# Windowed attention moved from stretches of its own into the slots of the expert stream, in a one-core hybrid block

## What is computed

```python
def attn_b(x, w_qkv, w_out, b_out):                    # H = 16 heads of 8, WINDOW = 64
    q, k, v = heads(split(x @ w_qkv.T))
    scores = q @ k.T / sqrt(8)
    allowed = (j <= i) & (i - j < WINDOW)
    attn = softmax(where(allowed, scores, -inf))
    return (attn @ v) @ w_out.T + b_out

def ffn(x):                                            # 32 experts, 8 of them weighted above zero per token
    w = normalised_top8(softmax(x @ gate_w.T))
    gate, up = split(x @ gate_up_w[e].T)               # 64 hidden features of each expert e
    return sum_e w[:, e] * ((silu(gate) * up) @ down_w[e].T)
```

## Time and profile before

| what | value |
|---|---|
| time, median of 3 runs (lowest, highest) | 999.18 us (999.04, 1001.05) |
| span of the profiled execution | 997.6 us |
| PE busy, share of the span | 911.7 us, 91% |
| DVE, ACT, POOL busy | 65%, 61%, 66% |
| the chain that ended last: PE, ACT, POOL, issue, DVE | 61%, 11%, 7%, 5%, 4% |

### The profile page before, as it was taken

How to read it: one execution, slowest core, us unless ns; L and a number is a source line. 1 busy time by engine, 2 the same in 40 slices (tenths; PEclk the granted TensorE clock), 3 DMA queues, 4 the chain that set the end, 5 groups by cost and what they waited for, 6 DMA issues and landing times.

```text
span 997.6 us, 16805 instructions
## 1 busy us (share of the span) xinstructions
PE 911.7 (91%) x5472; PEld 627.0 (63%) x5472; DVE 647.7 (65%) x1447; ACT 611.6 (61%) x1875; POOL 661.2 (66%) x610
## 2 busy tenths in 40 slices
PE   3267899899999999999999999999999998999998
PEld 1144566686666666586666666677666666657665
DVE  5886867688658638697739737787735347437432
ACT  4345566984664575895674575797455377386432
POOL 7676878657688649666759857756765545646554
PEclk8567999989999999999999999999999999999999
DMA  5005252014353524610433534520333560350452
GB/s 185 0 3 135 46 129 72 16 45 108 88 127 87 121 79 96 155 44 12 96 87 88 127 98 85 146 65 18 84 99 81 139 156 12 84 132 12 85 129 63
DMA packets 64762, 85.68 MB, mean 86 GB/s; under 512 B 5218, under 2 KB 30627, under 8 KB 64419
## 3 DMA queue, kind: packets, MB, share of 16 engines
q1 hardware_dynamic: 64674, 84.62, 35.2%
HBM read 79.32 MB, written 5.28 MB: 85 GB/s over the span
## 4 chain that ended last, share of the span: by engine, by line
PE 61%; ACT 11%; POOL 7%; issue 5%; DVE 4%; DVEq 0%; ACTq 0%; POOLq 0%
PE bank L1545 16%; PE bank L1522 8%; PE bank L1524 8%; PE bank L1523 8%; ACT probs L1089 5%; PE bank L1581 4%; PE bank L1566 4%; POOL work L881 3%; PE bank L1595 2%; PE bank L1559 1%; PE bank L1405 1%; POOL kv_terms L846 1%; DVE probsT L1345 1%; PE bank L1399 1%; POOL rstd L833 1%
## 5 line engine op out<-in xcount | busy, mean ns | idle before, releaser
L881 POOL TENSOR_TENSOR work<-work,spread_w 128x512 f32<-128x512 f32 x256 | 336.3, 1325 | 165.4 <-DVE work L1303 162.3
L1303 DVE TENSOR_TENSOR work<-work,bank 128x512 f32<-128x512 f32 x256 | 173.6, 681 | 214.0 <-ACT work L1064 128.1
L1545 PE MATMUL bank<-work,down_w 128*128 128x512 f32 x512 | 263.9, 599 | 9.3 <-POOL work L881 7.4
L1064 ACT ACTIVATE work<-bank 128x512 f32<-128x512 f32 x256 | 151.2, 596 | 182.1 <-PE bank L1524 178.6
L1089 ACT ACTIVATE probs<-bank,neg_max 128x96 f32<-128x96 f32 x512 | 166.0, 382 | 8.2 <-DVE neg_max L1331 5.7
L1522 PE MATMUL bank<-z_hi,gate_hi 128*128 128x512 f32 x256 | 167.0, 652 | 3.6 <-ACT elu L974 2.0
L889 POOL TENSOR_TENSOR probs<-probs,prob_inv 128x768 f32<-128x768 f32 x64 | 94.1, 1470 | 74.0 <-DVE prob_inv L1339 74.0
L1089 ACT ACTIVATION_READ_ACCUMULATOR probs<-bank,neg_max 128x1 f32 x512 | 125.6, 248 | 0.0
L1545 PEld LDWEIGHTS bank<-work,down_w 128*128 128x128 f32 x512 | 94.6, 189 | 40.5 <-POOL work L881 15.0
L1524 PE MATMUL bank<-z_hi,gate_lo 128*128 128x512 f32 x256 | 102.4, 400 | 0.0
L1522 PE MATMUL bank<-z_hi,up_hi 128*128 128x512 f32 x256 | 102.0, 398 | 0.0
(11 more groups left out here) (154 smaller groups left out, 1466.2 us busy)
## 6 DMA issues: line engine op xcount, KB each, us to landing
spread_w<-comb_dram SPq DMA_DIRECT2D x96, 512.0 KB, 6.7
spread_w<-comb_dram SPq DMA_DIRECT2D x128, 128.0 KB, 3.0
vals<-v_dram SPq DMA_DIRECT2D x16, 384.0 KB, 4.1
x_buf<-x SPq DMA_DIRECT2D x8, 256.0 KB, 3.4
v_dram<-v_tok SPq DMA_DIRECT2D x8, 256.0 KB, 4.5
out<-xs SPq DMA_DIRECT2D x8, 256.0 KB, 3.8
spread_w<-wg SPq DMA_DIRECT2D x1, 1024.0 KB, 6.5
spread_w<-wu SPq DMA_DIRECT2D x1, 1024.0 KB, 8.5
```

What stands on the lines that cost most here:

```text
L881: pool.tensor_tensor(work[:, n % WORK], work[:, n % WORK], spread_w[:, n // EACH % 2, s % EACH], ALU.mult).then_inc(hid_gated, 1)
L1064: act.activation(work[:, n % WORK], bank[GATE_BANKS[ring_of(row, f, s)]], ACT.Silu).then_inc(silu_ready, 1)
L1303: dve.tensor_tensor(work[:, n % WORK], work[:, n % WORK], bank[UP_BANKS[ring_of(row, f, s)]], ALU.mult).then_inc(gated_ready, 1)
L1545: pe.matmul(bank[Y_BANK], down_w[:, c], work[:, n % WORK], start=(c == 0), stop=(c == CH - 1)).then_inc(down_done, 1)
```

## The change

The attention stretches are gone. Each tile of attention B is cut into six parts, and a tile takes six consecutive slots of the stream, a new tile beginning every second slot: scores of head groups 0 and 1 with their maxima and the first group's exponentials; scores of groups 2 and 3, exponentials of groups 1 and 2, the first half's transpose; exponentials of group 3, the second half's transpose, the inverse sums; the first mixing phase; the second; the addition on POOL. Only row 0's tiles stand in eight slots without a chunk (`alone`), which take over that stretch's steps; rows 1 and 2 begin in slot 6 of `fourth`, row 3 in slot 4 of `third` and slot 9 of `fourth`. `PLAN` is re-timed around that.

Slots that hold attention (`HELD`, 71 of those with a chunk) use gate bank 4 and up bank 5 alone; the others keep the ring of three. In the 61 slots in which exponentials run, Silu becomes Tanh, which is in one table set with Exp: x·sigmoid(x) = 0.5·x·(1 + tanh(x/2)). In the 32 even ones (`SOFT`) DVE makes two instructions of it; in the 29 odd ones (`COPIED`) DVE makes one, ACT copies half the up bank out, and POOL multiplies by that copy before it multiplies by the weights.

Inside a tile, PE works with 32 x 32 tiles of its array (`tile_position` with four rows and four columns of tiles): scores take keys that are masked per head (`head_keys`) against 32 queries, so that a pair of groups is 8 masks and 8 products of 384 columns; and the mixing takes 24 products of 32 x 32 weights and 128 columns in each of two phases. DVE turns the probabilities itself in blocks of 32 x 32 (`dve.transpose`, 128 x 768, twice), so that PE's transposes and DVE's copies go. The probabilities stay unnormalised: DVE inverts the sums spread over features (128 x 128), PE transposes that, DVE copies it (`inv_turned`), and POOL multiplies the mixed values with it. The values come in 48 loads of 128 KB instead of 16 of 384 KB. Over the whole program PE loses 512 transposes and gains 32; table loads on ACT go from 65 to 56.

The diff, cut:

```diff
+RUNS = [((0, "alone", 0), 0, 0, TILES), ((1, "fourth", 6), 1, 0, TILES), ((2, "fourth", 6), 2, 0, TILES),
+        ((3, "third", 4), 3, 0, T), ((3, "fourth", 9), 3, T, TILES)]
...
+BESIDE = [{} for _ in TIMELINE]
+HELD, SOFT, COPIED = set(), [], []
+for run_start, run_row, run_first, run_end in RUNS:
+    for run_tile in range(run_first, run_end):
+        for stage_of_tile in range(6):
+            BESIDE[SLOT_AT[run_start] + 2 * (run_tile - run_first) + stage_of_tile][stage_of_tile] = run_row, run_tile
+for slot_at, (_, slot_place, slot_row, slot_f, slot_s) in enumerate(TIMELINE):
+    if any(k in BESIDE[slot_at] for k in range(5)):
+        HELD.add(slot_at)
+    if slot_place != "alone" and any(k in BESIDE[slot_at] for k in range(3)):
+        (COPIED if slot_s % 2 else SOFT).append(STAGE_AT[slot_row, slot_f] * CH + slot_s)
...
+        RING[slot_chunk] = 2
+        if slot_at not in HELD:
+            plain.append(slot_chunk)
+    if slot_at in HELD or slot_at == len(TIMELINE) - 1:
+        for back_to_end, plain_chunk in enumerate(reversed(plain)):
+            RING[plain_chunk] = (1, 0, 2)[back_to_end % 3]
...
+                if place == "alone":
+                    send_values(0, 1)
+                    load_windows(0, 2)
+                    next_weights(STAGE_AT[1, 0])
...
                 pool.wait_ge(gated_ready, n + 1)
-            def normalise(row, i, half):
-                pool.tensor_tensor(pr, pr, prob_inv[:, i % 2, part].unsqueeze(2).broadcast_to([P, HALF_BLOCKS, KW]),
-                                   ALU.mult).then_inc(probs_normed, 1)
+                if n in COPIED:
+                    pool.wait_ge(up_copied, COPIED.index(n) + 1)
+                    pool.tensor_tensor(inner, inner, up_copy[:], ALU.mult).then_inc(up_gated, 1)
+                    pool.wait_ge(up_gated, COPIED.index(n) + 1)
+                pool.tensor_tensor(inner, inner, weights, ALU.mult).then_inc(hid_gated, 1)
...
+                pool.wait_ge(mix_taken, 2 * tile(row, i) + 2)
...
+                pool.tensor_tensor(mixT[:, i], mixT[:, i], inv_turned[:], ALU.mult).then_inc(mix_picked, 1)
...
+                inner, gate = work[:, n % WORK], bank[GATE_BANKS[RING[n]]]
+                if n in SOFT or n in COPIED:
+                    act.activation(inner, gate, ACT.Tanh, scale=0.5).then_inc(silu_ready, 1)
+                else:
+                    act.activation(inner, gate, ACT.Silu).then_inc(silu_ready, 1)
+                if n in COPIED:
+                    act.wait_ge(up_ready, n + 1)
+                    wait(act, up_gated, COPIED.index(n))
+                    act.activation(up_copy[:], bank[UP_BANKS[RING[n]]], ACT.Copy, scale=0.5).then_inc(up_copied, 1)
...
+                    silu(row, f, s)
+                if 2 in BESIDE[at]:
+                    exponentials(*BESIDE[at][2], 3)
+                if 0 in BESIDE[at]:
+                    exponentials(*BESIDE[at][0], 0)
+                if 1 in BESIDE[at]:
+                    exponentials(*BESIDE[at][1], 1)
+                    exponentials(*BESIDE[at][1], 2)
...
+                if n in COPIED:
+                    dve.scalar_tensor_tensor(out=inner, in0=inner, scalar=1.0, in1=gate, op0=ALU.add,
+                                             op1=ALU.mult).then_inc(gated_ready, 1)
+                elif n in SOFT:
+                    dve.scalar_tensor_tensor(out=inner, in0=inner, scalar=1.0, in1=gate, op0=ALU.add,
+                                             op1=ALU.mult).then_inc(tanh_gated, 1)
+                    dve.wait_ge(tanh_gated, SOFT.index(n) + 1)
+                    dve.wait_ge(up_ready, n + 1)
+                    dve.scalar_tensor_tensor(out=inner, in0=inner, scalar=0.5, in1=up, op0=ALU.mult,
+                                             op1=ALU.mult).then_inc(gated_ready, 1)
+                else:
+                    dve.wait_ge(up_ready, n + 1)
+                    dve.tensor_tensor(inner, inner, up, ALU.mult).then_inc(gated_ready, 1)
...
-            def turned(row, i, blocks):
-                wait(dve, mix_ready, tile(row, i))
-                for b in blocks:
-                    dve.wait_ge(probsT_ready, tile(row, i) * NB + b + 1)
-                    dve.tensor_copy(probsT[:, b], bank[4 + b % 2][0:KW, :]).then_inc(probsT_copied, 1)
...
+                part = slice(half * HALF_HEADS, (half + 1) * HALF_HEADS)
+                dve.transpose(probsT[:, i % 2, part].rearrange("p h k -> p (h k)"),
+                              probs[:, part].rearrange("p h k -> p (h k)")).then_inc(probs_turned, 1)
...
+                dve.reciprocal(prob_inv[:].rearrange("p (h d) -> p h d", d=HD),
+                               prob_sum[:, i % 2].unsqueeze(2).broadcast_to([P, H, HD])).then_inc(inv_ready, 1)
...
+                if phase == 0:
+                    wait(dve, mix_picked, n)
+                    dve.tensor_copy(inv_turned[:], bank[LOW[0]][:, INV_COLS]).then_inc(inv_copied, 1)
+                    dve.wait_ge(inv_copied, n + 1)
+                heads = mix_all[:].rearrange("p (b j q) -> p b j q", b=NB, j=HG)
+                banks = quad[:, (LOW, HIGH)[phase][0]:(LOW, HIGH)[phase][1] + 1, 0:P].rearrange("p b (j q) -> p b j q", q=QB)
+                of_head = head_mask[:].unsqueeze(1).unsqueeze(3).broadcast_to([P, 2, HG, QB])
+                dve.tensor_tensor(heads[:, first:NB:2], banks, of_head, ALU.mult).then_inc(mix_taken, 1)
...
-                        mm = pe.matmul(bank[hg][:, KW * b:KW * (b + 1)],
-                                       qm[feats, i // T, NB * (i % T) + b].rearrange("p j q -> p (j q)"),
-                                       keysT[feats, first:first + KW], start=False, stop=(b == NB - 1),
-                                       tile_position=(QB * hg, 0), skip_group_check=True)
+                        pe.matmul(in_heads(hg, of_block), same_query[feats, 0],
+                                  window[feats, min(i, 1), b].unsqueeze(1).broadcast_to([QB, HG, KW]), start=True,
+                                  stop=False, tile_position=(QB * hg, QB * b), skip_group_check=True)
+                for b in range(NB):
+                    of_block, first = slice(QB * b, QB * (b + 1)), P * i + QB * b
+                    for hg in pair:
+                        feats = slice(QB * hg, QB * (hg + 1))
+                        mm = pe.matmul(in_heads(hg, of_block), queriesT[feats, first:first + QB],
+                                       head_keys[feats, :, first:first + KW], start=False, stop=True,
+                                       tile_position=(QB * hg, QB * b), skip_group_check=True)
                         if b == NB - 1:
...
-            def turn_probs(row, i, blocks):
...
+            def mix(row, i, phase):
+                n, banks = tile(row, i), (LOW, HIGH)[phase]
+                for k in banks:
+                    bank_free(k)
+                    emptied[k] = mix_taken, 2 * n + phase + 1
+                if phase == 0:
+                    pe.wait_ge(vals_loaded[i // 2 % 2], 16 * (KW // QB) * (n // 4 + 1))
+                    pe.wait_ge(inv_ready, n + 1)
+                    pe.transpose(bank[banks[0]][:, INV_COLS], prob_inv[:], ident[:])
+                    pe.wait_ge(probs_turned, 2 * n + 2)
...
+                        for k, b in zip(banks, PHASES[phase]):
+                            keys_of = slice(QB * b, QB * (b + 1))
+                            mm = pe.matmul(bank[k][QB * hg:QB * (hg + 1), 0:P].rearrange("p (j q) -> p j q", q=QB),
+                                           vals[keys_of, i // 2 % 2, past, i % 2, QB * hg:QB * (hg + 1)],
+                                           probsT[keys_of, i % 2, HG * hg:HG * (hg + 1), QB * past:QB * (past + 1)],
+                                           start=(past == 0), stop=(past == KW // QB - 1),
+                                           tile_position=(QB * b, QB * hg), skip_group_check=True)
```

798 lines of the change are left out of this document (322 added, 476 removed).

## The result

The changed kernel takes 1051.35 us (median; 1046.2 to 1063.04), the kernel before beside it 999.11 (997.75 to 1001.05): 1.049 times as long, 95% interval 1.0426 to 1.0554. The ratio leaves out the slowest run (1063.04 us, at a mean clock of 0.912 where the fastest had 0.927). The forecast was 974 and the range ended at 1028. The price of a tile on PE was nearly right; the steps that were only re-timed, the stretch alone and the waits beside the stream, with a lower clock behind them, were not.

What follows compares the result with a forecast made beforehand. PE was taken to bound the kernel. Removing the stretches left 784.8 us; adding 38 (lone slots), 115 (tiles on PE) and 34 (waits) gave 971.8 of span, 974 us measured, range 950 to 1028 (its own 950 to 994).

Steps and rivals of the forecast that it cites:

- PE's price of a tile: PE's work for one attention tile in the stream: 4.1 us against 6.15 before, 115 us for 28 tiles.
- the 0.10 of the sum: In PE's tile price, 0.10 us allowed for a change of tile shape; chosen, not measured.
- The prediction's bound of 0.06: Row 1's old stretch: PE idles 2.87 us in 48 shape changes, so 0.06 us each at most.
- Rivals 3: Only four array tiles run side by side on PE: 7.5 us a tile, about 1052 us; chance 0.05.
- the fourth rival: Every shape change on PE drains earlier products, 0.34 us each: 62 us more, 1036 us; chance 0.03.
- DVE's two unknown prices: On DVE, the 128 x 768 transpose taken at 0.91 us and the 128 x 128 reciprocal at 0.77.
- I take twice that share, 1.2 us a tile: Waits beside the stream: twice PE's old 5.3% loss in row 1's stretch, 34 us for 28 tiles.
- the first rival: Held slots: DVE's and ACT's queued steps enter the chain, 81 us lost instead of 34, 1021 us; chance 0.23.
- Its sign: PE idle over 2 us a tile in held slots, ending at bank 4 and 5 products, maxima or turned probabilities.
- The eight lone slots: Row 0's slots without a chunk: 38 us with values and weights loading behind, between 30 and 46.
- The old stretch's price: Row 0's lone slots costed at the old 6.15 us a tile: 4 x 6.15 + 11.7 = 36.3 us.
- Costed at nothing: No time given to table loads, ACT's copies, POOL's products, masked keys, extra loads, or steps re-timed in PLAN.

Runs made afterwards that it cites:

- the norms on POOL: Changed kernel with the scaling of seven norms in held slots moved from ACT to POOL: 1037.66 us, 1.0362.
- no copies: Changed kernel with the 29 odd slots made like the 32 even ones, so DVE makes two products and ACT copies no up bank: 1056.89 us.
- terms left out: Changed kernel without attention A's sums and products on DVE (22 instructions) for tiles whose steps stand in held slots: 1045.61 us.
- twelve exponentials: Changed kernel with the fourth head of each group left out, so ACT makes 12 exponentials a tile instead of 16: 1036.81 us.
- the tiles apart: Changed kernel with the tiles of rows 1 to 3 in slots without a chunk, apart from the stream: 1144.49 us, 1.1433.
- the best version: Changed kernel with moved PLAN steps, weights first on SP, steps ahead of mixing on PE, and seven norms on POOL: 1022.18 us, 1.0211.

## Why the prediction was wrong

1. *PE's price of a tile: near, 4.1 forecast and 4.5 measured.* PE's timeline from one slot's first gate pass (L1477) to the next one's, in a plain slot and in one with a score and a mixing piece, both without a wait or a step and at full clock:

```profile
315.86 0.80 PE L1477 MATMUL bank<-z_hi,gate_hi 128*128 128x512 f32 x1
...
318.10 0.80 PE L1477 MATMUL quad<-z_hi,gate_hi 128*128 128x512 f32 x1
```

```profile
468.28 0.50 PE L1477 MATMUL bank<-z_hi,gate_hi 128*128 128x512 f32 x1
...
469.87 0.35 PE L1518 MATMUL quad<-window,same_query 32*32 32x384 bf16 x8
470.04 0.83 PE L1525 MATMUL quad<-head_keys,queriesT 32*32 32x384 f32 x16
470.80 1.13 PE L1504 MATMUL bank<-work,down_w 128*128 128x512 f32 x2
471.85 0.94 PE L1545 MATMUL quad<-probsT,vals 32*32 32x128 f32 x48
472.72 0.50 PE L1477 MATMUL bank<-z_hi,gate_hi 128*128 128x512 f32 x1
```

A score piece takes 470.80 - 469.87 = 0.93 us, a mixing piece 472.72 - 471.85 = 0.87. But the slot takes 472.72 - 468.28 = 4.44 and the plain one 318.10 - 315.86 = 2.24, and 4.44 - 2.24 - 0.93 - 0.87 = 0.40 is left: about 0.10 for each of the four changes of shape in a slot, without a gap between records. A slot with a score piece alone, two changes, takes 3.38 (at 843.5 and 929.4 us), which leaves 0.21. With 0.1 to 0.3 for the sums' transpose, two slots make 4.5 to 4.7 a tile; over all held slots it is 4.5. So the 0.10 of the sum was the right size, but eight changes a tile cost it and the sum had five. The prediction's bound of 0.06 from PE's idle time could not see this, since the cost is not idle time. Rivals 3 (1.5 us for a mixing piece) and 4 (which decided from 0.19 a change) are refuted. The Trainium skill ("TensorEngine Tiling (Array Packing)", Key Properties) speaks of a drain at a change of tiling mode; the 0.10 a change may be that drain, and it is well under the 0.34 of the fourth rival.

2. *DVE's two unknown prices: near.* The lines of the whole run (count, busy us, mean ns, idle before):

```profile
L1308 DVE STREAM_TRANSPOSE probsT<-probs 128x768 f32<-128x768 f32 x64 | 62.1, 971 | 6.4 <-ACT probs L1062 6.0
L1315 DVE RECIPROCAL prob_inv<-prob_sum 128x128 f32<-128x128 f32 x32 | 29.1, 910 | 0.0
L1328 DVE TENSOR_TENSOR mix_all<-quad,head_mask 128x256 f32<-128x256 f32 x64 | 25.6, 400 | 4.7 <-PE quad L1545 3.6
```

The transpose was taken at 0.91, the reciprocal at 0.77, the half mix at 0.41: 0.25 us a tile too little, and within the bounds but for the reciprocal.

3. *"I take twice that share, 1.2 us a tile": too small, 1.6 measured.* With the stream's own 2.70 us a slot (before, 579.1 us outside the stretches and 22.7 for the ten chunks inside, over 223 chunks), 309 us leave 309 - 60 x 2.70 = 147 us for 24 tiles, 6.1 each where the forecast had 4.1 + 1.2 = 5.3. That is +20 us, a good half of it PE's price (4.5). The other 1.6 is lost time: some 1.2 of idle PE and 0.4 of half clock. Rows 1 and 2 lose 2.2 a tile, row 3, which has fewer steps there, 0.3. So the first rival's threshold of 2.1 is just reached where many steps stand, and its 3.45 nowhere. Its sign, over 2 us of idle PE a tile in these slots, did not come: the six rows above have 32 us, 1.3 a tile, and held slots came every 309 / 60 = 5.15 us, within the 4.9 to 5.5 that was to show the forecast right. Its reason held in part: the steps in DVE's and ACT's queues are no longer covered (the norms on POOL). That these engines are full did not hold (no copies, terms left out, twelve exponentials); a share of busy time cannot see who stands behind whom.

4. *The eight lone slots: "between 30 and 46, I take 38".* 45.9, at the upper end; with the eleven held slots behind them, which last 61.4 - 11 x 2.70 = 31.7 us longer than the stream's, row 0 takes 77.6 instead of 38 + 4 x 5.3 = 59.2: +18.5. The old stretch's price did not hold for the new tile: in `alone` PE waits 12.9 of the 45.9 us and is at half clock for 35. What a longer chain costs there and what the clock, no run separates.

5. *"Costed at nothing": the steps re-timed in `PLAN`.* The failed step that weighs most. The 152 plain slots take 446.3 us instead of 152 x 2.70 = 410: +36. The stages `second` took 41.0, 40.2 and 39.0 us before and take 46.4, 54.5 and 45.8. The second of these before:

```profile
509.00:549.20 40.20, 39.40 (x157) 26.79 (x156) 31.11 (x64) 21.94 (x40) 33.45 (x24) 1.00 0.40 91
```

In the change it is the row of 538.20 to 592.70 above, with 48.25 busy of 54.50 and clock 0.91. Most of the 36 is waiting: PE is idle 30.6 us in the plain slots, where 152 of the 213 chunks outside before's stretches would be idle 8.3 (11.6 in all), so 22; the clock costs some 4, and the rest, some 10, is more of PE's own work. With the tiles apart PE is idle 38 us in 213 such slots, 0.18 a slot against 0.20 in the change and 0.05 before, so it is not the tiles. That it is the new order of the steps is what remains; which steps, and how the old `PLAN` would do under the new tiles, was not tried. The prediction named this at its end as a thing that would make it wrong, but gave it no price and no chance.

6. *The clock: not in the sum at all.* Behind the lead-in it fell to half in ten places, in three before; the one at 425 us, behind the wait of 4.62 us, is typical. +28 us. It is part of points 3 to 5, and no loss beside them.

Together: 972 of span, -1.3 for the lead-in, +20, +18.5 and +36 give 1045, and the span is 1044.4.

What stays open is the remaining 21 us of the best version over the kernel before. They lie in row 0's stretches and the plain slots (PE idle 29 us there, still 21 over the 8.3). A `PLAN` in which those steps are spread out again was not tried.

## What to carry to other kernels

Before you move work into slots of another stream, write down for each instruction that someone waits for what now stands ahead of it in its own in-order queue; sums of busy time per slot don't show that, and a 0.23 us copy cost PE 4.6. Give steps that are only re-timed a price, from the stage where they land. And try repairs together: one wait taken away came back at the next one, all of them together brought 28 us.

## What the hardware showed that was not expected

- A change of shape on PE showed no gap and still cost about 0.10 us: a slot with four of them took 4.44 us where the plain slot and the two pieces by themselves make 2.24 + 0.93 + 0.87 = 4.04.
- Eight 32 x 32 tiles of the array seem to run side by side: 48 records of 128 columns in 0.87 us leave time for about six rounds of the 0.126 us that a round took before, not for the twelve of four tiles.
- Equal waits did not give equal clock. The same slots of row 3 took 49.6 us at clock 1.00 in one kernel and 59.6 at 0.80 in another with the same work there. Runs of the same kernel go with the clock: the changed kernel's spans are 1044.4, 1044.7, 1054.3 and 1061.2 us at mean clocks of 0.927, 0.928, 0.920 and 0.912. So a single profile of such a kernel tells a mechanism, and a gain of 5 us takes many runs.
- Keeping PE busy with filler brought the clock from 0.62 to 1.00 in the lone slots, and no time: 10.7 of the 45.0 us of the chain there were the filler's own.
